# Two routers of a four-layer network: first gathers issued in the router, top-two choice in two parts, probabilities on GpSimd, dense products in PE's waits

## The chip, the cores and the metric

The kernel is one program on one core of a Trainium2 chip. Its time is the device time of one execution in microseconds; smaller is better. Engines are named as the profile names them: PE (TensorE), DVE (VectorE), ACT (ScalarE), POOL (GpSimd), SP (SyncE, which issues DMAs).

## The reference

A network of four layers runs over 2048 tokens of 192 values (8 images of 256 tokens): window attention with an MLP, a Fourier block, landmark attention with a mixture of experts of which each token takes two, and full attention with a mixture of experts of which each token takes one. The change touches the two mixtures and what chooses the experts. Cut to that:

```python
# layer 2: two of eight experts
probs = jax.nn.softmax(flat @ router_w.T, axis=-1)
topk_probs, topk_idx = jax.lax.top_k(probs, 2)
importance = probs.sum(axis=0)
running = running + (1.0 - 0.9) * (importance - running) + 0.01
balanced = topk_probs / running[topk_idx]
balanced = balanced / balanced.sum(axis=-1, keepdims=True)
outs = second(silu(first(flat)))                       # by expert
combined = (sel * balanced[..., None]).sum(axis=1)
# layer 3: one of eight experts, at most C = 256 tokens for each
expert_gate, expert_index = max and argmax of softmax(xf @ router_w)
position_in_expert = cumsum(one_hot(expert_index)) * one_hot(expert_index)
out = gelu(gelu(x_e @ w1 + b1) @ w2 + b2) * gate, put back at each token
```

## The kernel before

The program is a sequence of blocks. In a block every engine has its own list of instructions, written out by hand, and waits for the others by semaphores; at the end of a block all engines meet at a barrier (the rows name it by L78), and POOL then clears the semaphores of the stage (L83). A block ends with a drain of POOL unless it is made with `drained=False`. Order on an engine is the order of the code; nothing schedules.

`route` is the router, called twice: as stage `l2r` with `top` 2 and as `l3r` with `top` 1. P is 128 partitions, NT is 16 tiles of 128 tokens, E is 8 experts, B is 8 images of TI = 2 tiles. In `l2r` the block first finishes landmark attention for each image: PE multiplies, DVE adds the residual and normalises (XN), PE turns XN (`turn`), ScalarE copies it to `xT` and stores it to `xn` in DRAM, and PE multiplies it with the router's weights into the bank `psL` (`logits`), 16 tiles of 8 logits side by side, 128 columns. In `l3r` the logits come ready in `front.psL`.

Then DVE works through one chain in which each operation waits for the one ahead (`link`): the largest logit (mx), the mask of the chosen expert (M, by way of EQ, W and m), for `top` 2 the same again on what is left (RK, best), their sum MT; PE counts with MT the tokens ahead (psU, psP), DVE forms each token's slot SI, its row LO and tile HI, and with them one-hot tables OH, OHT and OL[0], OL[1]. PE multiplies those into `psTab`, which holds for each slot its token; from it DVE makes `token_at`. The probabilities Pb are Z / den, with Z the exponentials; PE sums them (psI) for `imp`. POOL makes `tile_expert` in its own chain.

The experts follow in the next block. Stage `l2e` (`experts_any`) works on 20 pairs of slot tiles: POOL gathers the rows of a pair by `token_at` (`fetch`, two indirect DMAs) into X, a ring of RING = 4; PE turns them (`turn_tokens`), DVE copies them to XT, PE does the first layer, ScalarE the Silu, PE turns back and does the second layer. PE, which enters the block first by stepping eight semaphores, is followed by the others through these. Stage `l3e` (`experts_each`) does the eight experts with 256 rows each: `fetch`, `turn`, `hidden` (first layer with Gelu), `result_of`. `spare_xn` is a buffer of 128 x 1024 numbers that these stages do not use.

## Time and profile before

| | |
|---|---|
| runs before, median (lowest to highest) | 1106.94 us (1101.27 to 1108.46), 3 runs |
| the profiled execution, its own time | 1109.73 us |
| its span, first to last instruction | 1107.9 us |
| PE busy | 993.2 us, 90% |
| DVE, ACT, POOL busy | 579.9, 420.0, 282.7 us |
| mean granted clock of TensorE | 0.929 |

The profile is that of one execution. A row of the timeline gives the start, the busy time of the group, the engine, line, operation and tiles, and in brackets how long the engine had been idle before it and what ended that. The granted clock is 1.00 at 2.4 GHz and 0.50 at 1.2 GHz. Router `l2r` lies from 586 to 639 us, `l2e` behind it, `l3r` from 1003 to 1014 us, and `l3e` behind it up to the end.

### The profile page before, as it was taken

The page shows a single profiled execution, that of the slowest core. Times are in us where ns is not written, and L with a number is a line of the kernel's source. Part 1 is how long each engine was busy: PE and PEld are TensorE (multiplying, and loading weights), DVE is VectorE, ACT ScalarE, POOL GpSimd, SP SyncE. Part 2 cuts the span into 40 slices and gives each one's busy share as a digit, 9 for nine tenths or more (in the row PEclk, how much of TensorE's full clock was granted, in tenths as well). Part 3 has the DMA queues.
Part 4 walks back from the last instruction along what each step waited for, and adds up shares of the span by engine and source line. Part 5 has one row for each costly group of instructions (what it writes and reads, how often), then busy time and mean ns, then how long its engine had stood idle before and what let it go on. Part 6 is the DMA issues. An engine that isn't in the chain of part 4 may idle for free. (4 is left out here: it accounts for less than half of the span.)

```text
span 1107.9 us, 20470 instructions
## 1 busy us (share of the span) xinstructions
PE 993.2 (90%) x7510; PEld 754.8 (68%) x7511; DVE 579.9 (52%) x1396; ACT 420.0 (38%) x853; POOL 282.7 (26%) x397
## 2 busy tenths in 40 slices
PE   5998999999899999999899469999959799993996
PEld 5796878887656777887798336666647355562775
DVE  3844755553332674565656734444478477744122
ACT  3755254555323323443350011111137276641332
POOL 4663400111210211000002335555322211103242
PEclk9976999999999999999798679999969899995998
DMA  5555763420022400000008211112144433415660
GB/s 93 106 153 155 173 150 78 93 58 3 4 65 65 97 20 23 1 1 1 1 2 234 89 37 46 52 45 52 27 136 107 132 114 90 142 52 183 209 205 12
DMA packets 103318, 91.58 MB, mean 83 GB/s; under 512 B 25905, under 2 KB 95095, under 8 KB 102590
## 3 DMA queue, kind: packets, MB, share of 16 engines
q1 hardware_dynamic: 93221, 77.20, 25.6%
q0 software_dynamic: 5632, 11.07, 3.7%
q10 hardware_dynamic: 4377, 2.12, 0.7%
q8 instruction: 57, 0.93, 0.4%
q14 instruction: 31, 0.25, 0.1%
HBM read 64.44 MB, written 29.70 MB: 85 GB/s over the span
## 5 line engine op out<-in xcount | busy, mean ns | idle before, releaser
L1365 DVE TENSOR_REDUCE l0a_nmax<-l0a_psS 98x2 f32<-98x392 f32 x96 | 54.3, 567 | 41.5 <-PE l0a_psS L1176 32.8
L2944 ACT ACTIVATE l2e_H<-l2e_psH 128x512 f32<-128x512 f32 x40 | 21.7, 594 | 129.4 <-PE l2e_psH L2906 129.4
L922 ACT ACTIVATE l3a_PT<-l3a_psST 128x512 f32<-128x512 f32 x96 | 54.6, 595 | 31.3 <-PE l3a_psST L833 30.7
L1312 ACT ACTIVATE l0a_PT<-l0a_psST 98x392 f32<-98x392 f32 x96 | 47.2, 497 | 42.1 <-PE l0a_psST L1218 41.8
L2924 PEld LDWEIGHTS l2e_psY<-W2T,l2e_HT 128*128 128x128 f32 x320 | 51.5, 190 | 16.1 <-issue 16.0
L2867 POOL DMA_INDIRECT ys<-l2e_Y,result_of x40 | 41.9, 1048 | 71.4 <-DVE l2e_Y L2971 62.5
L2924 PE MATMUL l2e_psY<-W2T,l2e_HT 128*128 x320 | 57.3, 332 | 1.5 <-DVE l2e_Y L2971 0.7
L968 DVE TENSOR_REDUCE l3a_nmax<-l3a_psS 128x2 f32<-128x512 f32 x48 | 33.0, 687 | 24.5 <-PE l3a_psS L803 24.5
L2971 DVE COPY l2e_Y<-l2e_psY 128x384 f32<-128x384 f32 x20 | 11.2, 558 | 65.3 <-PE l2e_psY L2924 65.3
L2862 POOL DMA_INDIRECT l2e_X<-xn,token_at x40 | 39.3, 982 | 17.2 <-issue 17.2
L2903 PE MATMUL l2e_psH<-W1T,l2e_XT 128*128 x80 | 41.1, 638 | 2.8 <-issue 2.0
L833 PE MATMUL l3a_psST<-l3a_QS,l3a_KS 99*128 99x256 bf16 x192 | 36.4, 273 | 0.5 <-ACT l3a_PT L922 0.3
L968 DVE TENSOR_REDUCE l3a_nmax<-l3f_psL 128x2 f32<-128x512 f32 x48 | 32.9, 685 | 5.2 <-PE l3f_psL L803 5.1
L1314 ACT ACTIVATE l0a_PT<-l0a_psST 120x360 f32<-120x360 f32 x48 | 22.2, 471 | 31.7 <-PE l0a_psST L1226 29.2
L1649 PE MATMUL l0m_psY<-early,l0m_hT 128*128 128x192 f32 x192 | 32.2, 328 | 1.7 <-ACT l0m_hT L1676 1.7
L1368 DVE TENSOR_REDUCE l0a_nmax<-l0a_psS 120x1 f32<-120x312 f32 x48 | 22.9, 480 | 20.6 <-PE l0a_psS L1185 19.0
L1649 PEld LDWEIGHTS l0m_psY<-early,l0m_hT 128*128 128x128 f32 x192 | 31.1, 190 | 2.3 <-ACT l0m_hT L1676 2.3
L3140 PE MATMUL l3e_psY<-l3w_B,l3e_HT 128*128 128x192 f32 x192 | 32.5, 327 | 0.0
L1175 PE MATMUL l0a_psS<-first_KS,first_QS 96*98 96x196 bf16 x144 | 31.7, 258 | 0.7 <-DVE l0a_nmax L1365 0.4
L1143 POOL CAST l0a_mp<-l0a_nmax 128x20 bf16<-128x20 f32 x12 | 2.5, 208 | 115.9 <-DVE l0a_nmax L1368 115.9
L1676 ACT ACTIVATE l0m_hT<-l0m_psH,early 128x512 f32<-128x512 f32 x24 | 15.2, 684 | 43.8 <-PE l0m_psH L1639 43.8
L3140 PEld LDWEIGHTS l3e_psY<-l3w_B,l3e_HT 128*128 128x128 f32 x192 | 31.0, 190 | 0.3 <-issue 0.3
(602 smaller groups left out, 2704.0 us busy)
## 6 DMA issues: line engine op xcount, KB each, us to landing
l3w_A<-in_w SPq DMA_DIRECT2D x8, 771.0 KB, 4.6
l3w_B<-in_w SPq DMA_DIRECT2D x8, 672.0 KB, 5.5
l3a_QS<-qd SPq DMA_DIRECT2D x72, 64.0 KB, 2.3
l3a_KS<-kd SPq DMA_DIRECT2D x72, 64.0 KB, 2.4
rd<-l0r_p SPq DMA_DIRECT2D x24, 168.0 KB
first_QS<-qd SPq DMA_DIRECT2D x54, 64.0 KB
first_KS<-kd SPq DMA_DIRECT2D x54, 64.0 KB
W2T<-in_w2t SPq DMA_DIRECT2D x2, 1536.0 KB, 16.5
```

Source lines behind the costliest of these rows:

```text
L833: mm = nc.tensor.matmul(psST[item % 2][:, t * T:(t + 1) * T], KS[k % ring][:, s, key:key + P], QS[k % ring][:, s, u * T:(u + 1) * T], star ...
L922: nc.scalar.activation(PT[n % 3][:, s, :], psST[item % 2][:, :], ACT.Exp).then_inc(exp_done, 1)
L968: nc.vector.tensor_reduce(nmax[k % 2][:, TI * u:TI * (u + 1), s], psS[item % 2][:, :].rearrange("p (t k) -> p t k", t=TI), AX.X, ALU.max, ...
L1175: nc.tensor.matmul(o, q_[:, s, q], k_[:, s, keys], start=True, stop=False)
L1312: ex = nc.scalar.activation(PT[n % 3][0:WQ, s, :], psST[item % 2][0:WQ, 0:2 * W0], ACT.Exp)
L1365: mx = nc.vector.tensor_reduce(nmax[k % 2][0:WQ, 2 * j:2 * (j + 1), s], psS[item % 2][0:WQ, 0:2 * W0].rearrange("p (t k) -> p t k", t=2), ...
L1649: mm = nc.tensor.matmul(psY[a][:, t % 2 * C:(t % 2 + 1) * C], hT[p % 2][:, m, t * P:(t + 1) * P], Wd[:, m, :], start=(m == 0), stop=(m == ...
L2862: pool.indirect_dma_start(out=X[p % RING][:, t, :], out_offset=None, in_=G["xn"], in_offset=at(G["token_at"], 2 * p + t)).then_inc(x_in[p ...
L2867: pool.indirect_dma_start(out=G["ys"], out_offset=at(G["result_of"], 2 * p + t), in_=Y[p % RING][:, t, :], in_offset=None, bounds_check=2 ...
L2903: nc.tensor.matmul(psH[b][t][:, :], XT[b][:, t, :], W1T[:, 0, bass.ds(e * FI, FI)], start=True, stop=False)
L2924: mm = nc.tensor.matmul(psY[:, t * C:(t + 1) * C], HT[b][t][:, mb, :], W2T[:, bass.ds(e * NM + mb, 1), :].rearrange("p a c -> p (a c)"), s ...
L3140: mm = nc.tensor.matmul(psY[t][:, 0:C], HT[b][:, m, t * P:(t + 1) * P], W2[e][:, m, :], start=(m == 0), stop=(m == MF - 1))
```

## The change

Six edits. In `l2r` DVE's choice runs in two parts: on the logits of images 0 to 5 as soon as these are there, and on those of images 6 and 7, which PE now writes into the bank `psI`. The reciprocal of den moves ahead of the counting, and the product Z / den goes from DVE to POOL. In both routers POOL issues the gathers of the first pair, or of the first expert, inside the router's block, into `spare_xn`; the blocks end without a drain of POOL, and `l2e` and `l3e` fetch from the second on. PE gets dense products (`dense`: the identity as weights, 512 columns of X, the result unused) at its waits: in `l2r` 2, 8, 3, 3 and 5, in `l3r` 1, 6 and 5, at the start of `l2e` 3, at the start of `l3e` 3 and, behind the first turn, 2. In `l3e` the first layer of expert 0 comes ahead of the turn of expert 1.

```diff
+def spare_rows(G, n, width):
+    return [G["spare_xn"][:, u * 2 * width:(u + 1) * 2 * width].rearrange("p (t c) -> p t c", t=2) for u in range(n)]
+
+
+def gather_rows(nc, X, src, table, k, row_in):
+    nc.gpsimd.indirect_dma_start(out=X, out_offset=None, in_=src, in_offset=bass.IndirectOffsetOnAxis(ap=table[:, k:k + 1], axis=0)).then_inc(row_in, 16)
+
+
+def dense(nc, G, bank, n):
+    for c in range(n):
+        nc.tensor.matmul(bank[:, :], G["ident"][:, :], G["X"][:].rearrange("p t c -> p (t c)")[:, 0:512], start=True, stop=True)
+
+
+def route(nc, G, name, top, side, first_in, front=None):
...
-        block = st.block()
+        block = st.block(drained=False)
         flat = lambda g: g[:].rearrange("p t e -> p (t e)")
-        logits_of = psL[:, 0:NT * E].rearrange("p (t e) -> p t e", t=NT)
+        logits_of = lambda at: (psL if at.start == 0 else psI)[:, at.start * E:at.stop * E].rearrange("p (t e) -> p t e", t=at.stop - at.start)
+        parts = (slice(0, TI * (B - 2)), slice(TI * (B - 2), NT)) if top == 2 else (slice(0, NT),)
...
-                        mm = nc.tensor.matmul(psL[:, at:at + E], xT[i % 2][:, k, t * P:(t + 1) * P], RW[:, k, :], start=(k == 0), stop=(k == 1))
+                        mm = nc.tensor.matmul((psL if i < B - 2 else psI)[:, at:at + E], xT[i % 2][:, k, t * P:(t + 1) * P], RW[:, k, :], start=(k == 0), stop=(k == 1))
...
+            idle = psT[0] if top == 2 else psI
+            dense(nc, G, idle, top)
             pe.wait_ge(picked, 1)
...
                 pe.wait_ge(probs, 1)
                 nc.tensor.matmul(psI[:, 0:NT * E], ones[:, :], flat(Pb), start=True, stop=True).then_inc(imp_mm, 1)
+                dense(nc, G, idle, 8)
+                pe.wait_ge(low_done, 1)
+                dense(nc, G, idle, 3)
+            else:
+                dense(nc, G, idle, 6)
             pe.wait_ge(hot_done, 2)
             for k in range(top):
...
+                if k:
+                    dense(nc, G, idle, 3)
...
+            dense(nc, G, idle, 5)
...
+                pool.wait_ge(inverted, 1)
+                nc.gpsimd.tensor_tensor(Pb[:], Z[:], free(den[:, 0:1], [1, NT], [0, E]), ALU.mult).then_inc(probs, 1)
                 pool.wait_ge(base_done, 1)
...
+                pool.wait_ge(probs, 1)
+                pool.wait_ge(kept, 16 * B)
+                pool.wait_ge(slots_done, 2)
+                for t, X in enumerate(spare_rows(G, 1, C)[0][:, t, :] for t in range(2)):
+                    gather_rows(nc, X, G["xn"], G["token_at"], t, first_in)
...
+                pool.wait_ge(front.x_kept, 16 * (B // 2))
+                pool.wait_ge(front.xn_kept, 16 * (B // 2))
+                pool.wait_ge(slots_done, 1)
+                for t, X in enumerate(spare_rows(G, 1, 2 * C)[0][:, t, :] for t in range(2)):
+                    gather_rows(nc, X, G["xn3"], G["token_at"], t, first_in)
...
+            for at in parts:
+                dve.wait_ge(l_mm if top == 2 else front.l_mm, at.stop // TI)
+                t0, n = at.start, at.stop - at.start
+                link(V.tensor_reduce(mx[:, at], logits_of(at), AX.X, ALU.max))
+                src, src_max = logits_of(at), mx
+                for k in range(top):
+
+                    if k:
+                        link(V.scalar_tensor_tensor(RK[:, at], M[k - 1][:, at], -3e38, logits_of(at), ALU.mult, ALU.add))
+                        link(V.tensor_reduce(best[:, at], RK[:, at], AX.X, ALU.max))
+                        src, src_max = RK[:, at], best
+                    link(V.tensor_tensor(EQ[:, at], src, over_e(src_max, t0, n), ALU.is_equal))
+                    link(V.tensor_tensor(W[:, at], EQ[:, at], over_t(desc, n), ALU.mult))
+                    link(V.tensor_reduce(m[:, at], W[:, at], AX.X, ALU.max))
+                    if top == 2:
+                        link(V.tensor_tensor(M[k][:, at], W[:, at], over_e(m, t0, n), ALU.is_equal))
             if top == 2:
                 V.tensor_tensor(MT[:], M[0][:], M[1][:], ALU.add).then_inc(picked, 1)
             else:
...
-            V.tensor_tensor(Z[:], logits_of, over_e(mx), ALU.subtract).then_inc(shifted, 1)
+            for at in parts:
+                z = V.tensor_tensor(Z[:, at], logits_of(at), over_e(mx, at.start, at.stop - at.start), ALU.subtract)
+            z.then_inc(shifted, 1)
...
+            if top == 2:
+                V.reciprocal(den[:, :], den[:, :]).then_inc(inverted, 1)
...
-                    if top == 2:
-                        link(V.reciprocal(den[:, :], den[:, :]))
-                        V.tensor_tensor(Pb[:], Z[:], over_e(den), ALU.mult).then_inc(probs, 1)
...
-        X = [st.sb(f"X{r}", [P, 2, C]) for r in range(RING)]
+        X = spare_rows(G, 2, C) + [st.sb(f"X{r}", [P, 2, C]) for r in range(2, RING)]
...
-            for p in range(RING):
+            for p in range(1, RING):
...
+            dense(nc, G, psY, 3)
...
+        X = spare_rows(G, 1, 2 * C) + [st.sb(f"X{k}", [P, TI, 2 * C]) for k in range(1, D)]
...
-            pool.wait_ge(front.x_kept, 16 * (B // 2))
-            pool.wait_ge(front.xn_kept, 16 * (B // 2))
-            for e in range(D):
+            for e in range(1, D):
...
+            dense(nc, G, psY[0], 3)
             turn(0)
+            dense(nc, G, psY[0], 2)
+            hidden(0)
             turn(1)
-            hidden(0)
```

DVE in `l2r`, from the first largest logit to MT, before:

```order
L2696 TENSOR_REDUCE l2r_mx<-l2r_psL 128x16
L2704 TENSOR_TENSOR l2r_EQ<-l2r_psL,l2r_mx 128x128
L2705 TENSOR_TENSOR l2r_W<-l2r_EQ,early 128x128
L2706 TENSOR_REDUCE l2r_m<-l2r_W 128x16
L2708 TENSOR_TENSOR choice<-l2r_W,l2r_m 128x128
L2701 SCALAR_TENSOR_TENSOR l2r_RK<-choice,l2r_psL 128x128
L2702 TENSOR_REDUCE l2r_best<-l2r_RK 128x16
L2704 TENSOR_TENSOR l2r_EQ<-l2r_RK,l2r_best 128x128
L2705 TENSOR_TENSOR l2r_W<-l2r_EQ,early 128x128
L2706 TENSOR_REDUCE l2r_m<-l2r_W 128x16
L2708 TENSOR_TENSOR choice<-l2r_W,l2r_m 128x128
L2710 TENSOR_TENSOR l2r_MT<-choice 128x128
```

and the second part in the change, which stands behind the same eleven operations with 12 and 96 in the place of 16 and 128:

```order
L2735 TENSOR_REDUCE l2r_mx<-l2r_psI 128x4
L2743 TENSOR_TENSOR l2r_EQ<-l2r_psI,l2r_mx 128x32
L2744 TENSOR_TENSOR l2r_W<-l2r_EQ,early 128x32
L2745 TENSOR_REDUCE l2r_m<-l2r_W 128x4
L2747 TENSOR_TENSOR choice<-l2r_W,l2r_m 128x32
L2740 SCALAR_TENSOR_TENSOR l2r_RK<-choice,l2r_psI 128x32
L2741 TENSOR_REDUCE l2r_best<-l2r_RK 128x4
L2743 TENSOR_TENSOR l2r_EQ<-l2r_RK,l2r_best 128x32
L2744 TENSOR_TENSOR l2r_W<-l2r_EQ,early 128x32
L2745 TENSOR_REDUCE l2r_m<-l2r_W 128x4
L2747 TENSOR_TENSOR choice<-l2r_W,l2r_m 128x32
L2749 TENSOR_TENSOR l2r_MT<-choice 128x128
```

The eleven operations stand twice, once on 96 and once on 32 elements, and MT is one operation as before.

PE in `l2r`, from the last logits to the end of the block (rows of two waits in a row are merged), before:

```order
L2555 MATMUL l2r_psL<-early,l2r_xT 128x8 x8
L2587 MATMUL l2r_psU<-onesb,l2r_MT 128x128
L2588 MATMUL l2r_psP<-l2r_MT,tri 128x128
L2590 MATMUL l2r_psP<-earlier,l2r_TT 128x128
L2591 MATMUL l2r_psP<-earlier,l2r_TT 128x8
L2594 MATMUL l2r_psI<-choice,early 128x128
L2599 MATMUL l2r_psTab<-l2r_OHT,l2r_OL 128x40 x32
```

and in the change:

```order
L2570 MATMUL l2r_psI<-early,l2r_xT 128x8 x8
L2492 MATMUL l2r_psT<-X,ident 128x512 x2
L2604 MATMUL l2r_psU<-onesb,l2r_MT 128x128
L2605 MATMUL l2r_psP<-l2r_MT,tri 128x128
L2607 MATMUL l2r_psP<-earlier,l2r_TT 128x128
L2608 MATMUL l2r_psP<-earlier,l2r_TT 128x8
L2611 MATMUL l2r_psI<-choice,early 128x128
L2492 MATMUL l2r_psT<-X,ident 128x512 x11
L2623 MATMUL l2r_psTab<-l2r_OHT,l2r_OL 128x40 x16
L2492 MATMUL l2r_psT<-X,ident 128x512 x3
L2623 MATMUL l2r_psTab<-l2r_OHT,l2r_OL 128x40 x16
L2492 MATMUL l2r_psT<-X,ident 128x512 x5
```

The dense products (L2492) stand in the places where PE waits for MT, for the tables and for the end of the block; the last logits go to `l2r_psI`.

PE at the start of `l3e`, before; six more rows with the turn of experts 0 and 1 stand ahead of the first:

```order
L3112 MATMUL l3e_psX<-ident,l3e_X 128x128
L3112 MATMUL l3e_psX<-ident,l3e_X 64x128
L3126 MATMUL l3e_psH<-l3e_XT,l3w_A 128x256 x2
L3129 MATMUL l3e_psH<-l3e_XT,l3w_A 128x256 x2
L3126 MATMUL l3e_psH<-l3e_XT,l3w_A 128x256
L3126 MATMUL l3f_psL<-l3e_XT,l3w_A 128x256
L3129 MATMUL l3e_psH<-l3e_XT,l3w_A 128x256
L3129 MATMUL l3f_psL<-l3e_XT,l3w_A 128x256
```

and in the change, from behind the turn of expert 0:

```order
L2492 MATMUL l3e_psY<-X,ident 128x512 x2
L3165 MATMUL l3e_psH<-l3e_XT,l3w_A 128x256 x2
L3168 MATMUL l3e_psH<-l3e_XT,l3w_A 128x256 x2
L3165 MATMUL l3e_psH<-l3e_XT,l3w_A 128x256
L3165 MATMUL l3f_psL<-l3e_XT,l3w_A 128x256
L3168 MATMUL l3e_psH<-l3e_XT,l3w_A 128x256
L3168 MATMUL l3f_psL<-l3e_XT,l3w_A 128x256
L3165 MATMUL l3e_psH<-l3e_XT,l3w_A 128x256 x2
L3168 MATMUL l3e_psH<-l3e_XT,l3w_A 128x256 x2
L3151 MATMUL l3e_psX<-ident,l3e_X 128x128
L3151 MATMUL l3e_psX<-ident,l3e_X 64x128
```

The first layer of expert 0 (`l3e_psH`, `l3f_psL` from `l3w_A`) has moved ahead of the turn of expert 1 (`l3e_psX`).

## Rows read from the trace of the kernel before

**Rows 1.** Waits of PE, 585 to 680: line waited for: us in total, times, longest

```profile
PE l2r_psI L2594 <- DVE choice L2752: 8.7, 1, 8.7
PE l2e_psX L2892 <- DMA l2e_X<-xn,token_at: 6.6, 1, 6.6
```

**Rows 2.** Timeline, 609 to 672: start us, us, engine line op out<-in xcount [idle before]

```profile
615.18 0.96 PE L2555 MATMUL l2r_psL<-early,l2r_xT 96*128 96x8 f32 x8
...
620.11 0.29 DVE L2696 TENSOR_REDUCE l2r_mx<-l2r_psL 128x16 f32<-128x128 f32 x1 [4.18 <-PE l2r_psL L2555]
...
623.67 0.29 DVE L2710 TENSOR_TENSOR l2r_MT<-choice 128x128 bf16<-128x128 f32 x1
...
627.23 0.67 DVE L2732 TENSOR_TENSOR l2r_EQ<-l2r_RK,choice 128x128 f32<-128x128 f32 x1
627.84 1.02 POOL L2619 TENSOR_SCALAR l2r_te_cmp<-l2r_te_cmp 128x320 f32<-128x320 f32 x1
...
628.26 0.18 DVE L2734 TENSOR_SCALAR l2r_SI<-l2r_S 128x32 int32<-128x32 f32 x1
...
633.09 0.24 DVE L2751 RECIPROCAL l2r_den<-l2r_den 128x16 f32<-128x16 f32 x1
...
633.57 1.54 DVE L2755 TENSOR_TENSOR l2r_OHT<-l2r_OH,token 128x1280 f16<-128x1280 f16 x1
...
637.43 0.72 PE L2599 MATMUL l2r_psTab<-l2r_OHT,l2r_OL 128*128 128x40 f16 x16 [1.54 <-DVE l2r_OL L2748]
...
638.82 0.18 DVE L2769 TENSOR_SCALAR token_at<-l2r_te 128x40 uint32<-128x40 f32 x1
...
640.10 1.28 ACT L2944 ACT_TABLE_LOAD   x1 [15.59 <-PEq L2885]
...
640.58 1.23 POOL L2862 DMA_INDIRECT l2e_X<-xn,token_at  x1 [5.36 <-issue]
642.11 0.95 POOL L2862 DMA_INDIRECT l2e_X<-xn,token_at  x1 [0.30 <-issue]
...
644.77 0.69 PE L2892 MATMUL l2e_psX<-ident,l2e_X 128*128 128x128 f32 x2 [6.62 <-DMA l2e_X<-xn,token_at]
...
647.04 3.63 PE L2903 MATMUL l2e_psH<-W1T,l2e_XT 128*128 x4 [0.75 <-DVE l2e_XT L2954]
...
654.43 1.98 PE L2903 MATMUL l2e_psH<-W1T,l2e_XT 128*128 x4 [0.85 <-issue]
```

**Rows 3.** Windows: each engine's busy us (PE, PEld, DVE, ACT, POOL), clock, DMA share, GB/s

```profile
650.00:651.00 1.00, 1.00 (x3) 0.30 (x4) 0.00 (x0) 0.00 (x0) 0.69 (x2) 0.81 0.33 98
998.00:999.00 1.00, 0.70 (x4) 0.39 (x4) 0.68 (x3) 0.17 (x1) 0.32 (x1) 0.77 0.81 267
```

**Rows 4.** Timeline, 990 to 1040, router l3r and the experts behind it

```profile
998.09 0.70 PE L666 MATMUL l3a_psST<-ident,l3f_XN 128*96 128x128 f32 x4 [2.47 <-DVE l3f_XN L659]
...
1011.96 1.03 PE L2599 MATMUL l3r_psTab<-l3r_OHT,l3r_OL 128*128 128x64 f16 x16 [5.64 <-DVE l3r_OHT L2758]
1013.03 0.17 DVE L2771 TENSOR_SCALAR token_at<-l3r_psTab 128x16 uint32<-128x16 f32 x1 [1.13 <-PE l3r_psTab L2599]
...
1015.34 1.11 POOL L3083 DMA_INDIRECT l3e_X<-xn,token_at  x1 [6.64 <-issue]
...
1016.76 0.95 POOL L3083 DMA_INDIRECT l3e_X<-xn,token_at  x1 [0.30 <-issue]
...
1019.86 1.12 PE L3112 MATMUL l3e_psX<-ident,l3e_X 128*128 128x128 f32 x4 [6.86 <-DMA l3e_X<-xn,token_at]
...
1023.30 1.91 PE L3126 MATMUL l3e_psH<-l3e_XT,l3w_A 128*128 128x256 f32 x4
...
1029.49 0.70 PE L3126 MATMUL l3e_psH<-l3e_XT,l3w_A 128*128 128x256 f32 x2
...
1034.57 0.66 PE L3112 MATMUL l3e_psX<-ident,l3e_X 128*128 128x128 f32 x4
...
1035.61 0.83 DVE L3191 COPY l3e_XT<-l3e_psX 64x256 f32<-64x256 f32 x2
```

More of the change, by code:

```diff
@@ L3491, in one_expert @@
             weights = AllExperts(nc, ctx, self.w["w13"], self.w["w23"])
-            route(nc, G, "l3r", 1, weights, front)
-            experts_each(nc, G, weights, out, front)
+            fetched = ctx.enter_context(Stage(nc, "l3x"))
+            x_in = [fetched.sem(f"x_in{k}") for k in range(4)]
+            route(nc, G, "l3r", 1, weights, x_in[0], front)
+            experts_each(nc, G, weights, out, x_in, front)
 def build(nc, w, consts, out):
```

36 lines of the change are left out of this document (12 added, 24 removed).

## The prediction

> **What bounds the kernel now.** I read the waits of PE first. Around the router l2r the longest are one for the table of probabilities, 8.7 us, and one for gathered rows, 6.6 us [rows 1]. Then I read the timelines of both routers, to see which wait ends last. In l2r DVE carries the chain: the first of twelve linked operations starts at 620.11, when the last logits are done, and the last, MT, ends at 623.96; behind the second one-hot table PE's slot products start at 637.43, token_at is ready at 639.00, the two first gathers are issued at 640.58 and 642.11, and PE turns their rows from 644.77 on [rows 2]. The 8.7 us for the probabilities are not on that path: with them PE would only wait for the one-hot tables. In l3r token_at is ready at 1013.20, the gathers go at 1015.34 and 1016.76, PE turns from 1019.86 on, and the first layer starts at 1023.30 [rows 4]. Last I read the granted clock. It is back at 2.4 GHz only inside 650 to 651, and falls in 998 to 999 [rows 3], so PE's work on these paths runs at 1.2 GHz. Behind both routers PE's own work sets the pace, so a start that is sooner there moves the end one for one.
>
> **The profiled execution** took 1109.73 us, with a span of 1107.9; the median of the runs shown is 1106.94. I work out the sum on the profile and take it off both. A change under 1%, 11 us, is about what a measurement of this kernel cannot tell from no change.
>
> **Router l2r, the choice in two parts.** Twelve operations on 128 elements take 623.96 - 620.11 = 3.85 us, 0.32 each with the gap [rows 2]. The first part, 11 operations on 96 elements, needs only the logits of image 5, which end at 615.18 + 0.96 = 616.14. At 0.32 each, its ceiling, it is done by 619.7, before the last logits. Behind those remain 11 operations on 32 elements and MT. One on 32 elements took 0.18 [rows 2], 0.22 with the gap: 2.4 + 0.3 = 2.7 us. Gain 1.1 us (bounds 0.6, if reading PSUM costs more, and 1.4). Z comes in two pieces, and the reciprocal (0.24) now stands ahead of the table of tiles; both lie partly in waits for PE and ScalarE. I charge 0.15 (bounds 0 and 0.5).
>
> **Probabilities by GpSimd.** Reciprocal and product filled DVE from 633.09 to 633.57, on the chain: gain 0.48 us [rows 2]. On POOL the product stands ahead of the chain that makes tile_expert. The trace has no such product on POOL; the nearest row is 1.02 us for 320 elements, so I take 0.4, bound it by 1.0, and it hides: POOL was idle for 5.36 us ahead of its first gather. What can cost is the company: one DVE product took 0.67 us beside POOL's work, where the same shape, MT, takes 0.29 [rows 2]. One such loss is 0.38; I take 0.2 (bounds 0 and 0.8, two of them). The Trainium skill, GPSIMD Engine Reference, Key points, says that GpSimd shares its SBUF interfaces with VectorE, and that this touches DVE instructions with two SBUF inputs. Of the DVE operations next to the new product only `chosen` has two, so by the rule the loss is 0.38 at most, and the sum would change by less than 0.2; the slowed product, which reads two SBUF tiles, agrees with it.
>
> **Dense products.** A product of 512 columns has the shape of the first layer's: four took 3.63 us, mostly at 1.2 GHz, and 1.98 at 2.4 GHz [rows 2]. With the load of registers taken off I use 0.85 and 0.43 each. Behind the logits come two, 1.7 us, over before MT. Behind the probabilities come eight from about 625.5; they end between 628.9 and 632.3. The first one-hot table, which they must not pass, is ready at 633.1 - 1.4 = 631.7. I take the clock to be up before that: ahead of 650 PE had done five turns and four wide products, here it does more. Three more end at 633.4, when OHT is ready (633.57 + 1.54 - 1.85 = 633.3), and three more fit into the time of the second table. The sixteen products behind it took 0.72 at 1.2 GHz; I take 0.2 off (bounds 0 and 0.4). Five more run beside POOL's gathers.
>
> **Gathers inside the router.** token_at is ready at 639.00 - 1.1 + 0.15 - 0.48 + 0.2 - 0.2 = 637.6. POOL issues at 637.7 and, 1.53 us later, at 639.2; before it had needed 1.58 us from token_at to its first issue. By the 2.65 us from second issue to PE's start the rows are there at 641.9. But POOL now comes to the barrier only behind its second issue, at 640.2, and every engine waits for it there. Then PE steps eight semaphores; ScalarE, which waits for one of them, moved at 640.10, 1.1 us behind token_at [rows 2]. So PE starts three new products at about 641.1 and ends them at 642.4: turning starts 2.4 us sooner, held by PE's own filler, not by the rows. The turns gain 0.5 from the clock (four took 1.12 and 0.66 us at its two levels [rows 4]), the first layer 3.63 - 1.98 = 1.65. The rows of pair 1, issued from 641.6 on, are there at 645.8, and PE turns them at 647. Sum for l2r: 2.4 + 0.5 + 1.65 = 4.5 us (bounds 1.3 and 6).
>
> **Router l3r.** Here the choice is not split. One dense product, to 1004.6, is over before MT; six from 1006.4 at 0.85 end at 1011.5, just ahead of OHT, for which PE waits until 1011.96. The sixteen products took 1.03; I take 0.3 off (bounds 0 and 0.5). token_at is ready at 1012.9, the gathers go at 1013.0 and 1014.45, and by 3.1 us from second issue to start the rows are there at 1017.5. The barrier is passed at 1015.5 and three products end at 1017.1, so the rows are last: turning starts 2.3 us sooner. From a turn's start to the end of DVE's copies are 1036.44 - 1034.57 = 1.87 us at 2.4 GHz, so expert 0's first layer starts at 1019.6 instead of 1023.30; two more products run meanwhile. At 2.4 GHz a first layer takes 1034.57 - 1029.49 = 5.08 us; this one, with the clock low at first, took 6.19. It ends at 1024.7. Here the new order costs: expert 1 is turned now, and its first layer waits 1.87 us, where before it followed at once. It starts at 1026.6 instead of 1029.49 [rows 4]. Gain 2.9 us (bounds 1 and 3.5). From there PE does the same work at the same rate, and weights are asked for at the same points of it.
>
> **Sum.** 4.5 + 2.9 = 7.4 us: the profiled 1109.7 becomes 1102.3, the median 1106.9 becomes 1099.5.
>
> **Rivals.** First, the clock is lost again at the border behind l2r. In l3r it fell right behind 2.47 us in which PE stood idle [rows 3, 4]. Behind l2r PE ends its five products at about 638.6 and starts again at 641.1: 2.5 us, as long. Then the three products take 2.55, turning starts at 643.7, and the first layer is slow again: l2r gives 1.5 us instead of 4.5, in all 4.4, which is 1102.5. For it speaks the length of the idle time; against it, that the stretch ahead is dense.
>
> Second, slower than before: the dense products come late. If the clock stays at 1.2 GHz in both routers, the eight of l2r end at 632.3 and three more at 634.9, 1.6 behind OHT; with sixteen small ones and three more PE is at 638.2, 2.3 behind the second table (637.43 - 1.5); five more, past POOL, end at 643.2, and three behind the barrier at 646.6: 1.8 us later than 644.77. In l3r five end at 1017.3, three at 1020.1, expert 0 starts at 1022.4 at the old pace and expert 1, behind its turn, at 1030.5: 1.0 late. That is +2.8 us, 1109.7. It decides at whether the clock is up before PE comes to the slot tables. Against it speaks that the clock came back each time PE had wide work to do.
>
> Third, more than the sum. The mean clock of 0.929 over 1107.9 us is 157 us at half rate, of which 34 (616 to 650) and 27 (998 to 1025) lie at the routers; the other 96 can shift with the new start times, either way. With both upper bounds, 6 + 3.5, and 1.5 from there, the gain is 11 us: 1096.
>
> **Chances.** Forecast 0.64, clock lost at the border 0.20, late products 0.05, more than the sum 0.11. The runs before lay between 1101.3 and 1108.5, so two medians differ by some 2 us by themselves. The forecast's own bounds and the first rival with these 2 us make the range 1094.5 to 1106. Faster by over 1%: 0.11; within 1%: 0.86; slower by over 1%: 0.03.
>
> **What would show it.** In l2r: MT some 2.7 us behind the last logits, no DVE operation between first one-hot table and OHT, clock at 1.00 from about 629 on, PE's wait for gathered rows gone. In l3r: clock up before the turn of expert 0, PE idle some 1.2 us behind the turn of expert 1. The prediction is wrong if a stage outside both routers moves, if the gathered rows land later beside the barrier, if PE reaches OHT or a table after DVE, or if the clock reads 0.50 between the border of l2r and the first layer.

## The result, and the profile after

| | before | changed |
|---|---|---|
| median (lowest to highest), 20 runs each | 1106.06 us (1101.27 to 1109.19) | 1111.2 us (1105.93 to 1117.55) |
| profiled execution: time, span | 1109.73, 1107.9 us | 1105.93, 1104.1 us |
| mean granted clock in it | 0.929 | 0.955 |

The ratio is 1.0048, 95% interval 1.0034 to 1.0063: by it 5.3 us slower (the medians differ by 5.1), where 7.4 us faster was predicted, and outside the range. One execution of the changed kernel took 4827 us and is left out of the ratio; without it the median is 1110.9. The profiled execution is the fastest of its twenty, so the two spans must not be compared; stretches inside them must.

Waits of PE in the changed kernel, 578 to 675 us (line waited for: us in total, times, longest), against [rows 1]:

```profile
PE l2e_psY L2492 <- issue: 1.7, 1, 1.7
...
PE l2r_psI L2611 <- POOL choice L2634: 0.8, 1, 0.8
...
PE l2r_psU L2604 <- DVE l2r_MT L2749: 0.6, 1, 0.6
```

Both long waits are gone: 8.7 us for the probabilities became 0.8, and no wait for gathered rows is left. That looks like success, but a wait is also gone when PE comes too late to wait. The timeline of l2r shows it, against [rows 2] (start us, us, what, in brackets the idle time ahead and what ended it):

```profile
608.79 0.26 DVE L2735 TENSOR_REDUCE l2r_mx<-l2r_psL 128x12 f32<-128x96 f32 x1 [0.25 <-PE l2r_psL L2570]
...
609.08 1.91 PE L2570 MATMUL l2r_psI<-early,l2r_xT 96*128 96x8 f32 x16
...
610.84 3.40 PE L2492 MATMUL l2r_psT<-X,ident 128*128 128x512 f32 x4
...
611.99 0.19 DVE L2735 TENSOR_REDUCE l2r_mx<-l2r_psI 128x4 f32<-128x32 f32 x1
...
614.46 0.29 DVE L2749 TENSOR_TENSOR l2r_MT<-choice 128x128 bf16<-128x128 f32 x1
...
616.04 0.41 POOL L2634 TENSOR_TENSOR choice<-l2r_Z,l2r_den 128x128 f32<-128x128 f32 x1 [8.20 <-DVE l2r_den L2760]
...
616.83 9.96 PE L2492 MATMUL l2r_psT<-X,ident 128*128 128x512 f32 x22
...
617.95 0.67 DVE L2775 TENSOR_TENSOR l2r_EQ<-l2r_RK,choice 128x128 f32<-128x128 f32 x1
...
623.81 1.54 DVE L2795 TENSOR_TENSOR l2r_OHT<-l2r_OH,token 128x1280 f16<-128x1280 f16 x1
...
625.27 2.33 DVE L2791 TENSOR_TENSOR l2r_OL<-count,l2r_LO 128x2048 f16<-128x2048 int32 x1
...
626.62 0.56 PE L2623 MATMUL l2r_psTab<-l2r_OHT,l2r_OL 128*128 128x40 f16 x16
...
627.03 2.82 PE L2492 MATMUL l2r_psT<-X,ident 128*128 128x512 f32 x6
...
629.68 0.56 PE L2623 MATMUL l2r_psTab<-l2r_OHT,l2r_OL 128*128 128x40 f16 x16
...
630.09 4.54 PE L2492 MATMUL l2r_psT<-X,ident 128*128 128x512 f32 x10
...
630.93 0.18 DVE L2809 TENSOR_SCALAR token_at<-l2r_te 128x40 uint32<-128x40 f32 x1
...
632.05 1.23 POOL L2487 DMA_INDIRECT spare_xn<-xn,token_at  x1 [4.34 <-DVE token_at L2809]
...
633.58 0.95 POOL L2487 DMA_INDIRECT spare_xn<-xn,token_at  x1 [0.30 <-issue]
...
636.28 2.81 PE L2492 MATMUL l2e_psY<-X,ident 128*128 128x512 f32 x6 [1.65 <-issue]
...
638.93 0.38 PE L2933 MATMUL l2e_psX<-ident,spare_xn 128*128 128x128 f32 x2
```

The second part of the choice takes 2.76 us (614.75 - 611.99), the whole choice took 3.85 before. But in this profile the second part starts 1.0 us late: the last logits end at 610.99, and DVE is busy with the first part up to 611.96. So MT ends 3.8 us behind the last logits, 3.9 before. In the two other profiles of the changed kernel the second part starts 0.11 us behind the last logits, and MT ends 2.9 us behind them. (The first profile's last logits are the faster ones, 1.91 us at the higher clock, so less of the first part hides behind them.)

The two dense products ahead of MT stand in the trace as x4 and take 3.40 us, mostly at 1.2 GHz, and the eleven behind the probabilities as x22: each product is two matmul records. The 22 take 9.96 us, 0.905 us a product, with the clock up:

```profile
616.00:617.00 1.00, 0.50 (x3) 0.50 (x4) 0.86 (x5) 0.00 (x0) 0.41 (x1) 1.00 0.00 0
...
622.00:623.00 1.00, 1.00 (x4) 0.52 (x3) 1.00 (x1) 0.00 (x0) 1.00 (x1) 1.00 0.00 0
```

(Windows: start:end, length, busy us of PE, PEld, DVE, ACT, POOL, then the granted clock, here 1.00, and the DMA share and GB/s.) OHT is ready at 625.35, PE's slot products start at 626.62; the second OL is ready at 627.60, its products start at 629.68. Both tables wait for PE, 1.27 and 2.08 us, without a bracket that says so. The five products behind them end at 634.63, as late as POOL's second gather (634.53), and three more end when turning starts, at 638.93: 5.35 us behind the start of the second gather, where before it was 2.66 [rows 2]. From the last mx to the first turn it is 26.9 us, before 24.7 [rows 2].

The timeline of l3r in the changed kernel, against [rows 4]:

```profile
1002.63 5.95 PE L2492 MATMUL l3r_psI<-X,ident 128*128 128x512 f32 x12
...
1008.42 0.64 PE L2623 MATMUL l3r_psTab<-l3r_OHT,l3r_OL 128*128 128x64 f16 x16
...
1008.89 4.54 PE L2492 MATMUL l3r_psI<-X,ident 128*128 128x512 f32 x10
...
1010.11 1.11 POOL L2487 DMA_INDIRECT spare_xn<-xn,token_at  x1 [4.96 <-DVE gate_at L2817]
...
1013.84 2.81 PE L2492 MATMUL l3e_psY<-X,ident 128*128 128x512 f32 x6 [0.42 <-PEq L78]
...
1016.49 0.60 PE L3151 MATMUL l3e_psX<-ident,spare_xn 128*128 128x128 f32 x4
...
1025.55 0.70 PE L3165 MATMUL l3e_psH<-l3e_XT,l3w_A 128*128 128x256 f32 x2 [1.27 <-DVE l3e_XT L3232]
```

From first gather to first turn it is 6.38 us, before 4.52 [rows 4]: five products carry PE to the barrier at 1013.43, three more to 1016.49. PE is in time for OHT here. The new order's wait for DVE's copies is there, 1.27 us.

The third place is one that the change does not touch. DVE's waits at the start of l3p, 785 to 840 us, changed kernel:

```profile
DVE X L3360 <- DMA l3p_Y<-ys: 1.3, 1, 1.3
```

The kernel before has no such row in its first two profiles, and one of 0.7 us in a third.

### The profile page after: what moved, and what is told of

It reads as the page before. It is cut to its first block and busy times, and to the rows that moved or that the text cites. A ratio compares the mean times of both kernels' runs of the same rounds, so it can differ in the third digit from the quotient of the medians.

```text
span 1104.1 us, 20654 instructions
## 1 busy us (share of the span) xinstructions
PE 1019.3 (92%) x7592; PEld 762.3 (69%) x7593; DVE 581.4 (53%) x1407; ACT 420.0 (38%) x853; POOL 284.7 (26%) x398
## 5 line engine op out<-in xcount | busy, mean ns | idle before, releaser
L1365 DVE TENSOR_REDUCE l0a_nmax<-l0a_psS 98x2 f32<-98x392 f32 x96 | 54.3, 567 | 41.3 <-PE l0a_psS L1176 32.8
L922 ACT ACTIVATE l3a_PT<-l3a_psST 128x512 f32<-128x512 f32 x96 | 54.6, 595 | 32.1 <-PE l3a_psST L833 31.5
L968 DVE TENSOR_REDUCE l3a_nmax<-l3f_psL 128x2 f32<-128x512 f32 x48 | 32.8, 684 | 5.2 <-PE l3f_psL L803 5.2
L1314 ACT ACTIVATE l0a_PT<-l0a_psST 120x360 f32<-120x360 f32 x48 | 22.2, 471 | 31.7 <-PE l0a_psST L1226 29.2
L1649 PE MATMUL l0m_psY<-early,l0m_hT 128*128 128x192 f32 x192 | 32.2, 328 | 1.7 <-ACT l0m_hT L1676 1.7
L3179 PE MATMUL l3e_psY<-l3w_B,l3e_HT 128*128 128x192 f32 x192 | 32.5, 327 | 0.0
L1175 PE MATMUL l0a_psS<-first_KS,first_QS 96*98 96x196 bf16 x144 | 31.7, 258 | 0.6 <-DVE l0a_nmax L1365 0.3
L845 PE MATMUL l3a_psO<-l3a_PT,Vall 128*32 128x256 f32 x384 | 30.5, 391 | 0.0
```

The source lines that it names most:

```text
L845: mm = nc.tensor.matmul(psO[k % 2][32 * s:32 * s + 32, u * T:(u + 1) * T], V[:, tile, GQ * (k % HG) + s, :], PT[n % 3][:, s, t * T:(t + 1) ...
L922: nc.scalar.activation(PT[n % 3][:, s, :], psST[item % 2][:, :], ACT.Exp).then_inc(exp_done, 1)
L968: nc.vector.tensor_reduce(nmax[k % 2][:, TI * u:TI * (u + 1), s], psS[item % 2][:, :].rearrange("p (t k) -> p t k", t=TI), AX.X, ALU.max, ...
L1175: nc.tensor.matmul(o, q_[:, s, q], k_[:, s, keys], start=True, stop=False)
L1365: mx = nc.vector.tensor_reduce(nmax[k % 2][0:WQ, 2 * j:2 * (j + 1), s], psS[item % 2][0:WQ, 0:2 * W0].rearrange("p (t k) -> p t k", t=2), ...
L1649: mm = nc.tensor.matmul(psY[a][:, t % 2 * C:(t % 2 + 1) * C], hT[p % 2][:, m, t * P:(t + 1) * P], Wd[:, m, :], start=(m == 0), stop=(m == ...
```

## The experiments

All are compared with runs of the kernel before on the same chip. Of each profile I read five stretches: **A**, from the start of the last mx in l2r to PE's second turn in l2e; **B**, from l2e's last product to l3p's first; **P**, l3p's first to l3a's first; **C**, from there to mx in l3r; **D**, from that mx to the first product of expert 0's second layer. Behind D PE needs the same 63.8 us to its last instruction in all six profiles of the two kernels. The last mx starts at most 0.11 us behind the last logits everywhere but in the changed kernel's first profile, where it is 1.0 us; counted from the last logits its A would be 32.5. Where a kernel has one profile, its five stretches are those of a single execution, while the ratio is that of 5 or more.

| kernel | ratio [95%] | A | B | P | C | D |
|---|---|---|---|---|---|---|
| before, three profiles | 1 | 31.5, 31.7, 31.8 | 13.3, 13.1, 13.9 | 53.4, 53.5, 53.3 | 135.6, 137.2, 136.5 | 31.4, 32.2, 32.4 |
| changed, three | 1.0048 [1.0034, 1.0063] | 31.5, 31.8, 31.8 | 14.5, 15.0, 14.9 | 54.3, 54.3, 54.3 | 137.7, 137.2, 137.3 | 31.2, 31.5, 31.4 |
| no dense product | 0.9981 [0.9961, 1.0000] | 30.3 | 13.1 | 54.1 | 136.1 | 32.2 |
| 256 columns | 0.9976 [0.9956, 0.9996] | 26.9 | 14.6 | 53.0 | 138.5 | 29.0 |
| 8 columns | 1.0028 [1.0008, 1.0047] | 30.0 | 14.6 | 53.2 | 137.3 | 32.8 |
| 22 of 512 | 0.9965 [0.9944, 0.9986] | 27.0 | 13.2 | 54.0 | 141.4 | 29.7 |
| 22 of 256 | 0.9991 [0.9976, 1.0006] | 30.3 | 13.2 | 54.3 | 140.2 | 30.4 |
| 22 of 512, 13 of 8 | 1.0007 [0.9988, 1.0026] | 33.9 | 14.9 | 53.0 | 140.6 | 29.7 |
| choice only | 0.9988 [0.9972, 1.0004] | 30.0 | 13.1 | 53.6 | 135.4 | 31.5 |
| 256, old gathers | 1.0032 [1.0018, 1.0046] | 30.6 | 14.6 | 54.5 | 138.2 | 32.5 |
| before + 35 of 8 | 1.0092 [1.0064, 1.0121] | 36.7 | 14.9 | 54.5 | 136.7 | 33.4 |
| before + 70 of 8 | 1.0124 [1.0104, 1.0144] | 45.0 | 13.4 | 53.8 | 135.6 | 34.8 |
| before + 5 in the wait | 1.0022 [1.0005, 1.0039] | 31.7 | 13.1 | 53.6 | 139.9 | 30.9 |
| before + 11 in the wait | 1.0022 [1.0003, 1.0040] | 31.6, 31.8 | 13.8, 13.2 | 53.0, 53.6 | 139.9, 138.8 | 32.3, 31.5 |
| before + 17 in the wait | 1.0017 [0.9999, 1.0035] | 32.3 | 13.2 | 53.8 | 142.7 | 31.4 |

**No dense product.** `dense` issues nothing; the rest of the change stays.

```diff
-    for c in range(n):
+    for c in range(0):
```

> The change without any dense product (all 35 left out; the computation stays whole). Theory A: each dense product is two matmuls, 0.91 us at 2.4 GHz and about 1.8 us at 1.2 GHz, so it costs twice what I took, and PE comes to OHT, to the second table and to the turn of the first rows after the others; in a typical execution, where the clock comes back later than in the one profiled, by several us more. Then this kernel loses the delay and is faster than the change by 6 to 9 us, and faster than before by 1 to 4 us (1102 to 1105): split choice 1.1, POOL's product 0.5, gathers 0.5 and 1, at the old clock. Rival B: the dense products do no harm, and what makes the change slower is the rest (gathers inside the block, blocks without a drain, the new order of the first layer). Then this kernel is slower than before by more than the change is, since it lacks the clock: 1112 or more.

Measured: 1103.7 us against 1105.6, 7.4 us below the changed kernel by the ratios. The dense products are what makes the change slow.

**Products of 256 columns.** Half the filler in every place.

```diff
-        nc.tensor.matmul(bank[:, :], ... [:, 0:512], start=True, stop=True)
+        nc.tensor.matmul(bank[:, 0:256], ... [:, 0:256], start=True, stop=True)
```

> The change with 256 columns in each dense product instead of 512, in the same places and number. Theory A (each product costs twice what I took): at 256 columns it costs the 0.43 to 0.45 us at 2.4 GHz of my sum, PE is at OHT and at the tables before DVE, and the forecast comes true but for the 1.1 us that POOL takes between token_at and its first gather: 1100 to 1103, or some 9 us faster than the change. If half the columns don't bring the clock back, it lies with the kernel without dense products, 1102 to 1105. Rival B (the rest makes it slower): as slow as the change, 1109 to 1113.

Measured: 1102.37 against 1105.6. Its PE timeline in l2r:

```profile
617.61 5.51 PE L2492 MATMUL l2r_psT<-X,ident 128*128 128x256 f32 x16
624.46 1.56 PE L2492 MATMUL l2r_psT<-X,ident 128*128 128x256 f32 x6 [1.35 <-DVE l2r_OL L2791]
625.93 0.57 PE L2623 MATMUL l2r_psTab<-l2r_OHT,l2r_OL 128*128 128x40 f16 x16
...
628.19 0.57 PE L2623 MATMUL l2r_psTab<-l2r_OHT,l2r_OL 128*128 128x40 f16 x16 [0.30 <-DVE l2r_OL L2791]
...
634.67 0.44 PE L2933 MATMUL l2e_psX<-ident,spare_xn 128*128 128x128 f32 x2 [0.47 <-DMA spare_xn<-xn,token_at]
```

Now PE waits for DVE again, and for the rows. A is 4.8 us shorter than the mean of before (31.7), D 3.0 us shorter (32.0). The forecast had 4.5 and 2.9. Five products take 2.40 us at 2.4 GHz in this trace, 0.48 each. So with products near the price that it had assumed, its mechanism holds in both routers. The whole kernel still gains only 2.7 us by the ratio: in the profiled execution B and C are longer than before.

**The changed kernel and the kernel before once more.** No edit.

> The changed kernel once more, for the trace of another execution. Its runs lay between 1106 and 1118 us, and the one profiled was the fastest. Theory A: a slower execution shows the clock coming back later in one of the routers, and the time by which PE is late at OHT, the second table or the first turn grows with it, 3 us or more over the 1.3, 2.1 and 2.7 us of the profile seen. Rival B: the routers take as long as in the first profile, and the difference lies in other stages.

> The kernel before once more, for a second trace. What stages outside both routers differ between this and the first trace of before is no effect of the change. If spells of lowered clock move about between executions, as between the traces of before and of the change (a spell of 7.5 us in l2p in one, none in the other), stages differ here by up to 5 us too.

Measured: 1115.36 and 1111.45 us, one execution each. The slower execution of the changed kernel was expected to show PE later at the tables; it does not, PE is late at OHT by 1.27 and at the second OL by 2.08 us in all three profiles. It is late at MT as well in the two later ones: the counting products start 0.5 us behind MT. The table shows that A, B and P of a kernel repeat within 0.8 us. What does not repeat lies ahead of the last logits: the first product of l2r starts at 586.0, 585.1 and 579.9 us in the profiles of before, at 579.6, 586.9 and 586.1 in those of the changed, and from there to the last logits it is 34.1 us in the four late ones and 31.4 in the two early ones.

**Products of 8 columns.** As many instructions, next to no columns (`bank[:, 0:8]`, `[:, 0:8]`).

> The change with 8 columns in each of its 35 dense products: the same instructions, next to no work. In the traces of the two kernels with wide dense products PE's start in l3p lies 14.5 us behind the end of l2e, in those without 13.1 to 13.3; there a load of instructions falls together with the first reads of ys, in which DVE waits 1.8 us for l3p_Y. Theory C: the further instructions on PE shift the loading of code, here by some 10 us, and the price of 1.4 us hangs on their number: this kernel shows 14.5 us there, no gain from the clock in the routers, and is 1 to 3 us slower than the kernel without dense products (1103.7): 1105 to 1107. Rival D: the price hangs on the work of the products (the clock afterwards), then the gap is 13.1 to 13.3 us and the time that of the kernel without them, 1103 to 1104.5.

Measured: 1107.53 against 1106.0, 1.0028; slower than with none (0.9981). A is not longer than before, B is, by 1.2 us.

**Choice only.** No dense product, gathers, drain and order as before.

> Only the choice in two parts, the reciprocal ahead and the product on POOL; no dense product, gathers, drains and the order of the first layer as before. From the traces: MT 1.1 us sooner, OHT a further 0.5, in all 1.6 us less from the last logits to token_at, and no change in l3r. Theory: 1104 us, 1.6 us faster than before, within what can be told. Rival: POOL's product, whose table of experts ends later too, holds DVE up beside it, and nothing is gained: 1105.6.

Measured: 1105.71 against 1106.0. A is 1.7 us shorter: 1.1 for the choice, 0.55 for the product on POOL. In the whole time that is within what can be measured.

**256 columns, old gathers.** Half-width filler, gathers issued in the experts' block, with the drain; the new order stays. Gathers and drain go back together, so the run does not tell them apart.

> The change with 256 columns in each dense product, but the first gathers issued in the experts' block, as before, and the blocks drained; new order of the first layer kept. It tells what the gathers inside the router are worth under a clock that is up. In the trace with half columns token_at to the turn of the first rows took 5.05 us, before 5.77, so the gathers should be worth 0.7 us in l2r and (5.4 against 6.7) 1.3 us in l3r. Theory: 2 us slower than the same kernel with its gathers inside (1102.4): 1104.4. Rival: without them the barrier opens sooner and POOL's first issue is no later, then the same 1102.4 or better.

Measured: 1109.57 against 1106.0. A is 3.7 us longer than with the gathers inside (26.9), D 3.5 (29.0), where 0.7 and 1.3 were expected. Its timeline:

```profile
631.92 0.18 DVE L2799 TENSOR_SCALAR token_at<-l2r_te 128x40 uint32<-128x40 f32 x1
...
635.05 1.23 POOL L2892 DMA_INDIRECT spare_xn<-xn,token_at  x1 [4.34 <-issue]
...
639.20 0.44 PE L2923 MATMUL l2e_psX<-ident,spare_xn 128*128 128x128 f32 x2 [2.68 <-DMA spare_xn<-xn,token_at]
```

POOL issues 2.95 us behind token_at instead of 0.94: all engines meet at the barrier first, and PE comes there behind its filler. That is 2.1 us up to the first turn. The other 1.6 us of A lie behind it, where the clock was lost again after PE had been idle for 2.68 us:

```profile
642.00:643.00 1.00, 1.00 (x2) 0.45 (x2) 0.49 (x1) 0.00 (x0) 0.70 (x2) 0.50 0.36 97
```

This is the prediction's first rival, in the kernel whose rows come late. In these runs the filler pays only together with the gathers inside.

**22 products instead of 35.** In l2r 1, 5, 1, 1 and 3, in l3r 1, 5 and 2, then 1 in l2e and 1 and 1 in l3e. Two of the edits:

```diff
-                dense(nc, G, idle, 8)
+                dense(nc, G, idle, 5)
...
-            dense(nc, G, idle, 5)
+            dense(nc, G, idle, 3 if top == 2 else 2)
```

> The change with 22 dense products of 512 columns in place of 35: 1, 5, 1, 1, 3 in l2r, 1 ahead of l2e, 1, 5, 2 in l3r, 1 and 1 in l3e, so that at 0.91 us each they end before what PE waits for. Theory A (the price of a product was off by two and PE was late): the routers give the 4 to 5 and 2 to 3 us that they gave with half the columns, and the time is 1101 to 1103. By theory C the gap behind l2e may be 13.1 or 14.5, since the number of instructions differs again. Rival D (wide products cost time elsewhere): no faster than the kernel without them, 1103.7 or more.

Measured: 1102.45 against 1106.0, the lowest ratio of all (that of 35 half-width products is within its interval), 3.9 us faster than before and 9 than the changed kernel. A is 4.7 us shorter than before, D 2.3. PE waits for DVE at both tables and for the rows:

```profile
620.95 7.98 PE L2492 MATMUL l2r_psT<-X,ident 128*128 128x512 f32 x12
629.27 0.57 PE L2623 MATMUL l2r_psTab<-l2r_OHT,l2r_OL 128*128 128x40 f16 x16 [0.34 <-DVE l2r_OHT L2795]
...
638.12 0.44 PE L2933 MATMUL l2e_psX<-ident,spare_xn 128*128 128x128 f32 x2 [0.63 <-DMA spare_xn<-xn,token_at]
```

B is back at 13.2. Its C is 4 to 6 us longer than before's; in part of it, where before reads 1.00, its clock was down:

```profile
984.00:985.00 1.00, 1.00 (x7) 0.93 (x6) 0.69 (x1) 0.00 (x0) 0.00 (x0) 0.50 0.00 0
```

**Small products alone, 35 and 70.** The kernel before, with nothing of the change but products of 8 columns at its eight places.

```diff
+            dense(nc, G, idle, top)
             pe.wait_ge(picked, 1)
...
+                dense(nc, G, idle, 11)
             pe.wait_ge(hot_done, 2)
```

> The kernel before, with nothing of the change but 35 products of 8 columns at the 8 places where the change has its dense products. Theory of the price and of the code loading (C: the number of PE instructions decides where the loading of PE's instructions falls, and a load that falls into the first reads of ys holds DVE there): the time from the last product of l2e to the first of l3p is 14.5 us as in the four kernels with 35 products, not 13.1 as in the kernels with none or 22; the routers stay as before within 0.5 us; the time is 1.0014 to 1.004 of before. Rival (the 1.4 us have their cause in what else the change does, its orders or its block without a drain): 13.1 us there, and a ratio of 1.000 within 0.001.

> The same with 70 products of 8 columns. If a place in the instruction stream decides (C), then the load lies elsewhere once more: the 14.5 us at the start of l3p need not stay, and the time can lie on either side of the run with 35. If instead each added instruction costs by itself, the ratio is twice as far from 1 as with 35, about 1.005 to 1.008, and no single place shows it.

Measured: 1115.25 (6 executions) and 1120.55 (5) against 1106.79. My expectation for the routers was wrong: a product of 8 columns is not free. PE in the run with 35:

```profile
628.96 4.70 PE L2484 MATMUL l2r_psT<-X,ident 128*128 128x8 f32 x22
633.51 0.69 PE L2611 MATMUL l2r_psTab<-l2r_OHT,l2r_OL 128*128 128x40 f16 x16
```

Eleven take 4.70 us, 0.43 each, and here they stand between the late probabilities and the tables. A is 5.0 us longer, with 70 13.3. But B does what the theory says that the place in PE's stream of instructions decides, and not what a price for each instruction would do: 14.9 with 35, 13.4 with 70, where DVE does not wait for ys.

**22 of 256 columns.**

> The kernel with 22 dense products, each of 256 columns, 5 us of filler less. Theory of the price: with 22 wide ones PE is already in time at every table, so nothing is gained in the choice's chain, and the clock may come back later; the time is that of the run with 22 wide ones, 0.996 to 0.999 of before. Rival (what is left of the filler still holds the barrier or the rows): 1 to 3 us faster than that run, 0.994.

Measured: 1105.05 against 1106.79. With half the filler of the 22 wide ones the gain in A is mostly gone (30.3, as with none): the clock stayed low from 617.5 to 651.6 us but for 631.2 to 634.6.

**22 of 512 and 13 of 8 columns.** The small ones stand behind l2r's last logits.

> The kernel with 22 dense products of 512 columns, and 13 of 8 columns behind the last logits of l2r, so that PE's instructions up to the third layer's end are as many as in the change. C: the time from l2e's last product to l3p's first is again 14.5 us, not 13.2, and the kernel is 1.5 to 4 us slower than the one with 22. Rival (a matter of how much PE does, not of its instructions): 13.2 us and the time of the one with 22, 0.9965 of before.

Measured: 1109.04 against 1106.79. A is 6.8 us longer than with 22 alone, and 4.1 of it is a place ill chosen: the 13 hold the counting products, and OHT ends 17.5 us behind the last logits instead of 13.4. The stretch that was asked for is B. DVE's waits for ys at the start of l3p (the run with 22 alone has no such row):

```profile
DVE X L3361 <- DMA l3p_Y<-ys: 1.8, 1, 1.8
```

It is 14.9 us, against 13.2, for 13 products in another stage. The median is 4.7 us above that of the run with 22, by the ratios; the two causes together would make more, so it does not price the stream by itself.

**The stream moved, the routers not: 5, 11 and 17 small products in the wait for the probabilities.** The kernel before, and:

```diff
+                for c in range(5):
+                    nc.tensor.matmul(psT[0][:, 0:8], G["ident"][:, :], ... [:, 0:8], start=True, stop=True)
                 pe.wait_ge(probs, 1)
```

> The kernel before with 5 products of 8 columns in l2r, in the 8.7 us in which PE waits for the probabilities; at 0.43 us each they take 2.2 us of that wait and nothing else. C (the place in PE's instruction stream decides where its loading falls): both routers stay as before within 0.3 us; the time from l2e to l3p is 13.1 or 14.5 to 14.9 us, according to where the load falls, and l3a may move by 1 to 2 us; ratio 0.999 to 1.004, and not the same for 5, 11 and 17 products. Rival (the stream costs nothing; what the kernels with small products lost was their own time in the routers): ratio 1.000 within 0.001 for all three.

> The same with 11 products, 4.7 us of the wait. C: as for 5, with 13.1 or 14.5 to 14.9 us from l2e to l3p, ratio between 0.999 and 1.004. Rival: 1.000 within 0.001.

> The same with 17 products, 7.3 us of the wait, still inside it. C: close to the 24 products that the change has up to there, so 14.5 to 14.9 us from l2e to l3p, ratio 1.001 to 1.004. Rival: 1.000 within 0.001.

Measured: 1108.77, 1108.15 and 1108.23 against 1106.46, all about 2 us slower, the intervals just above or at 1. The three share one set of 29 executions of the kernel before, so they are not three independent proofs. A is as before for 5 and 11, 0.6 longer for 17, D as before. B is 13.1 to 13.8, so the price that I expected there is absent, and the forecast of 14.5 or more with 17 failed. What is longer in the profiled executions is C. That the moved stream is what makes them slower is not shown.

**Second and third profiles,** of the kernel with 11, before and changed.

> The kernel with 11 small products in l2r's wait, profiled once more. If the moved stream costs its 2 us in l3a, the time from l3a's first product to mx of l3r is again above 139 us (139.9 in its first profile; 135.6 and 137.2 in those of before). If that stage only varies from one execution to the next, it can be anything from 135 to 142 here too.

> The kernel before, profiled a third time. If the stream decides, l3a to mx takes 135 to 137.5 us again; if the stage only varies, a value above 139 can come here as well. From l2e to l3p 13.1 to 13.3 us in either case.

> The changed kernel, profiled a third time. From l2e to l3p 14.5 to 15 us again, if the loading of PE's instructions falls there by its place in the stream; l3a to mx 137 to 138 us as in its two others, if that too is set by the stream. The routers as before: first turn of l2e 5.3 us behind the second gather, 6.4 us from first gather to first turn in l3r.

Measured: 1103.98, 1103.59 and 1114.45 us. C is 138.8 for the kernel with 11, a little below the 139 that I had set and above all three of before. In the third profile of before C is 136.5, as expected, but B is 13.9, where at most 13.3 was. B and P of the changed kernel repeat (14.9, 54.3), and so do its routers (5.36 and 6.38 us).

## Why the prediction was wrong

**The step that failed is the price of a dense product,** "With the load of registers taken off I use 0.85 and 0.43 each". It took "four took 3.63 us, ... and 1.98" [rows 2] for four products; the rows count matmul records, and a product is two of them (the first layer of a pair is two products of 512 columns in the code). The real prices are about twice those: 0.905 us at 2.4 GHz, and 1.7 at mostly 1.2 GHz. With 0.905 the eight and three behind the probabilities take 10 us and cannot end before OHT, whatever the clock. With half-width products or 22 wide ones PE is in time, and A + D is 7.8 or 7.0 us shorter than before, where the changed kernel's is 0.6 us shorter. So this step accounts for some 6.8 of the 12.7 us between forecast and result.

**The rival that came closest had 0.05.** "the dense products come late" is what happened, but its deciding point was wrong: "whether the clock is up before PE comes to the slot tables". The clock rose 3.2 to 3.6 us behind the last logits in the three profiles (at 614.6, 624.4 and 623.4), sooner than the 9 us of the forecast, and PE was late at OHT by the same 1.27 us in all three. At the true price PE is late without that condition. The rival's sum, 2.8 us slower in the two routers, did not come: the first turn of l2e is 2.3 to 2.6 us later than before, but the clock that is up makes the work behind it shorter by as much. The kernel is slower by more than the rival said, and for other reasons, so that it had the sign right is in part luck.

**What held.** MT 1.1 us sooner: 1.0 in two profiles of three, 0.1 in the first, where DVE's first part was not over before the last logits. Reciprocal and product off DVE 0.48: 0.55. POOL's product 0.4 us: 0.41, and no DVE operation beside it was slowed; but `chosen` started at 616.46, just as it ended, so the case that the prediction feared did not arise. The DVE operation of 0.67 us had been so before [rows 2], beside a product of 320 elements on POOL; its twin with the same inputs, 0.65 us ahead of it, took 0.29 beside a small one. The clock up before the border and not lost there: up; the first rival (0.20) did not come in the changed kernel. The wait for the copies behind the turn of expert 1 in l3r: 1.27 us. And the sum of both routers, at half width: 4.8 and 3.0 us against 4.5 and 2.9.

**Smaller misses.** POOL issues its first gather 0.94 us behind token_at (630.93 + 0.18 to 632.05), not 0.1. In l3r the filler ahead of the barrier ends behind POOL's own work there (1013.43 against 1012.48), so the barrier too is PE's. The prediction's 1019.6 for the first layer of expert 0 should be 1019.4 by its own terms (1017.5 and 1.87), and its range 1095.4 to 1106.6; neither changes the outcome.

**"From there PE does the same work at the same rate"** holds behind the routers in the strict sense (63.8 us behind D), but not between them. Means of three profiles each: A 31.7 and 31.7, D 32.0 and 31.4, that is 0.6 us gained where 7.4 were expected (0.2 if A is counted from the last logits); B 13.4 and 14.8, P 53.4 and 54.3, C 136.4 and 137.4, that is 3.3 us lost where nothing was changed. Together 2.7 us slower (3.1 from the last logits), of the 5.3 of the ratio.

**What the 1.4 us of B are.** The page of the profile lists two queues named "instruction", 8 and 14. With 24 products added, the packet of queue 8 near the end of l2e comes sooner (16.8 us ahead of that end, 12.0 without), that of queue 14 does not (13.3 us ahead in both the changed kernel and the one without dense products). I take queue 8 for the one that loads PE's instructions. A block of it, one packet of 0.02 MB, falls into the first reads of ys in the changed kernel, 798 to 805 us:

```profile
q1 hardware_dynamic: 2018, 1.46, 70.4%
q8 instruction: 1, 0.02, 0.8%
```

and in the kernel before the same stretch of l3p (803 to 810 us) has none:

```profile
q1 hardware_dynamic: 891, 0.65, 34.0%
q0 software_dynamic: 96, 0.00, 0.8%
```

Its three profiles have that packet 23.0 to 23.8 us behind the end of l2e, past l3p's first product. In every kernel with 24 or 25 added products ahead of l3p, of 8, 256 or 512 columns, with or without the rest of the change, the packet starts 6.8 to 7.2 us behind l2e's end, DVE waits 1.3 to 1.8 us for ys and B is 14.5 or more (eight profiles). In the other twelve, with 0, 5, 11, 12, 17 or 48 products, it starts 16.4 us or more behind and DVE does not wait, but for 0.7 us in one of the three of before and 0.6 in one of the two with 11. So a wait of up to 0.7 us comes without the packet. The Trainium skill, Runtime: NRT & Kernel Launch, Instruction fetch mechanics, says that an engine's instructions are refilled in blocks of 16 KiB, 256 instructions, and that the cost of a boundary is mostly hidden. The packet's size agrees, 0.02 MB. By that figure, as an estimate from the page, the 24 products with two records and two weight loads each move the boundary by 96 of 256. Whether the cost is hidden from PE these views do not tell; what grows beside the packet is DVE's wait for data.

That the packet's coincidence goes with B is shown; that it is the packet which delays the reads, and not something else that the length of the stream moves, is argued from it. Its own time is 1.1% of 16 engines in 800 to 805 us, that is 0.9 us of one engine, less than the wait.

**P and C are not explained by it.** P is 53.0 to 54.5 over all kernels and does not go with B: 54.1 in the kernel without dense products, 53.0 to 53.2 in three kernels with the packet in the reads. The 1.0 us of C is no more than its spread in the kernel before (135.6 to 137.2).

**What stays open.** 2.6 us of the 5.3 is in none of these stretches. C is 138.2 to 142.7 in nine profiles, those of the kernels with 22 products, with 5, 11 or 17 small ones, and with 35 of 256 columns (either place of the gathers), and 135.4 to 137.7 in the other eleven. It goes with the clock: the mean granted clock of C is 0.89 to 0.95 in the nine and 0.96 or 0.97 in ten of the eleven. The eleventh is the second profile of before, 0.94 and 137.2 us, which was low from 881.9 to 888.7:

```profile
884.00:885.00 1.00, 1.00 (x4) 0.41 (x3) 0.81 (x2) 0.15 (x2) 0.00 (x0) 0.50 1.01 135
```

So such a spell of low clock comes without any change, too. In the runs with 17 small and with 22 wide products the clock also fell near the end of l3a some 12 us sooner, counted back from mx of l3r, than before. With 17, windows of l3a read

```profile
983.00:984.00 1.00, 0.81 (x10) 0.27 (x10) 0.00 (x0) 1.00 (x3) 0.75 (x2) 1.00 0.00 0
991.00:992.00 1.00, 1.00 (x8) 0.99 (x6) 0.00 (x0) 0.74 (x2) 0.00 (x0) 0.50 0.00 0
```

and before it was still at 1.00 at 993, and fell at 998 [rows 3]. Whether the stream or chance of the execution sets these spells, one or two profiles of a kernel cannot tell.

## What to carry to other kernels

Count the records of a shape against the products in the code before a duration becomes a price: here one f32 product of 512 columns was two records, and all the filler was twice as dear. Size filler so that the engine is seen waiting, by however little, at each place where others depend on it: a wait that vanishes from the list can mean that the engine is late. And compare an unchanged stage between the traces: B grew in every kernel with 24 or 25 products added ahead of it, whatever their width. Fewer and wider fillers (22 of 512 columns, 0.9965) did better than 35 of 8 (1.0028) and as well as 35 of 256 (0.9976, intervals overlap).
